# State-space scan: u written in the place of h, third banks of psX and psW, state sums for four units at a time

## The reference, cut to what matters

```
xz = x @ in_proj.T;  xc, z = split(xz)              # 512 inner channels
xs = silu(causal_conv4(xc) + conv_b)
dt_r, B, C = split(xs @ x_proj.T)                   # 16 + 16 + 16
dt = softplus(dt_r @ dt_proj.T + dt_b)
a = exp(dt[..., None] * A)                          # 16 states for a channel
u = dt[..., None] * B[:, :, None, :] * xs[..., None]
h[t] = a[t] * h[t-1] + u[t]                         # along the 2048 steps of a row
y = sum_s(h * C) + xs * D_skip;  y = y * silu(z)
out = y @ out_proj.T
```

## Time and profile before

| | |
|---|---|
| median of 3 runs | 3406.47 us (3404.86 to 3411.97) |
| the profiled execution | 3401.26 us, span 3399.5 us |
| busy over the span | PE 94%, DVE 82%, ACT 68%, POOL 47% |
| state-space loop, 2296 to 3382 us | PE 1034.9, DVE 980.6, ACT 782.2, POOL 888.5 us busy of 1086.0 |
| mean granted clock of TensorE | 0.977 of full speed |

### The profile page before, as it was taken

One profiled execution on the slowest core, in us unless ns is written; L12 is line 12 of the kernel. 1 busy time (PEld: TensorE's weight loads), 2 busy tenths in 40 slices (PEclk: granted clock), 3 DMA queues, 4 the chain that ended last, 5 costly groups with the idle time before them and its releaser, 6 DMA issues. The chain is left out here.

```text
span 3399.5 us, 61118 instructions
## 1 busy us (share of the span) xinstructions
PE 3188.7 (94%) x19814; PEld 1279.1 (38%) x19815; DVE 2788.6 (82%) x4945; ACT 2316.7 (68%) x3660; POOL 1601.0 (47%) x2080
## 2 busy tenths in 40 slices
PE   7997999989999999999999999769999999999987
PEld 4654666632222222222222222343334334333333
DVE  6766334689999999999999999258899989898997
ACT  4444333358887887888788788657877767777763
POOL 2113300024444434444333444207888888888885
PEclk9999999989999999999999999889999999999998
DMA  5442211111111110111111010141222222222221
GB/s 169 131 151 91 78 56 53 48 42 29 53 45 40 39 34 27 31 36 36 36 33 34 25 34 27 46 136 59 69 75 81 71 73 69 73 87 66 76 78 50
DMA packets 160889, 211.63 MB, mean 62 GB/s; under 512 B 32324, under 2 KB 108364, under 8 KB 160604
## 3 DMA queue, kind: packets, MB, share of 16 engines
q1 hardware_dynamic: 141340, 172.51, 16.6%
q0 software_dynamic: 8512, 18.76, 1.8%
q10 hardware_dynamic: 10752, 16.78, 1.5%
HBM read 154.48 MB, written 52.69 MB: 61 GB/s over the span
## 5 line engine op out<-in xcount | busy, mean ns | idle before, releaser
L1439 ACT ACTIVATE prob<-psS 128x1024 f32<-128x1024 f32 (+3 forms) x1280 | 1104.0, 906 | 280.2 <-PE psS L1623 270.8
L1489 DVE TENSOR_REDUCE pmax<-psR 128x1 f32<-128x512 f32 x1674 | 1057.2, 684 | 79.9 <-PE psR L1565 47.6
L2265 POOL TENSOR_TENSOR hc<-h_d,crep 128x512 f32<-128x512 f32 x512 | 647.7, 1273 | 186.8 <-DVE h_d L2494 136.5
L1565 PE MATMUL psR<-kslab,qslab 48*128 48x512 bf16 (+3 forms) x2480 | 653.0, 352 | 22.2 <-DVE pmax L1489 14.0
L1638 PE MATMUL psVo<-prob,vaug 128*32 128x512 f32 (+3 forms) x5120 | 630.8, 546 | 1.5 <-ACT ov L1443 0.8
L1623 PE MATMUL psS<-qslab,kslab 51*128 51x512 bf16 (+3 forms) x2560 | 533.4, 353 | 39.8 <-ACT prob L1439 22.6
L2494 DVE TENSOR_TENSOR_SCAN h_d<-a,state,psU 128x512 f32<-128x512 f32 x384 | 489.4, 1275 | 0.0
L1354 POOL TENSOR_SCALAR_AFFINE_SELECT prob<-prob 128x256 f32<-128x256 f32 (+1 forms) x512 | 214.0, 421 | 533.1 <-ACT prob L1439 533.1
L2484 DVE TENSOR_TENSOR psU<-dtx,psX 128x512 f32<-128x512 f32 x512 | 356.0, 695 | 89.6 <-PE psX L2644 38.8
L1565 PEld LDWEIGHTS psR<-kslab,qslab 48*128 48x128 bf16 x2480 | 187.3, 94 | 628.9 <-DVE pmax L1489 473.6
L2397 ACT ACTIVATE a<-dt,a_neg 128x512 f32<-128x512 f32 x512 | 366.7, 723 | 54.5 <-DVE h_d L2494 53.6
(11 more groups left out here) (351 smaller groups left out, 5045.5 us busy)
## 6 DMA issues: line engine op xcount, KB each, us to landing
crep<-c_rows_d SPq DMA_DIRECT2D x256, 256.0 KB, 3.1
x_e<-rows_d SPq DMA_DIRECT2D x72, 128.0 KB, 2.0
y_d<-y SPq DMA_DIRECT2D x72, 128.0 KB, 1.7
q_d<-parts SPq DMA_DIRECT2D x48, 128.0 KB, 2.4
k_d<-parts SPq DMA_DIRECT2D x48, 128.0 KB, 2.3
qslab<-q_d SPq DMA_DIRECT2D x60, 96.0 KB
kslab<-k_d SPq DMA_DIRECT2D x60, 96.0 KB
wg<-n_L_ffn_gate_proj_w_dram ACTq DMA_DIRECT2D x8, 512.0 KB, 4.1
```

The lines of the kernel that those rows point to most:

```text
L1439: act.activation(prob[g % BUFS][:, :, off:BLK], psS[g % 2][:, :, off:BLK], ACT.Exp).then_inc(prob_ready, 1)
L1489: dve.tensor_reduce(into[:, lo:lo + (count - 1) * NEXT + 1:NEXT], psR[at % BANKS][:, 0:count * w].rearrange("p (n w) -> p n w", w=w), AX.X ...
L1565: ins = pe.matmul(dst[:, m * w:(m + 1) * w], qslab[u][rows, i * P:(i + 1) * P], kslab[u][rows, ch * BLK:ch * BLK + w], start=(m == 0), sto ...
L2265: pool.tensor_tensor(hc[:, g % CR], h[:, g % HR], crep[:, g // PAIR % SPR], ALU.mult).then_inc(hc_ready, 1)
```

## The change

- u is written into the ring place of h (SBUF) in place of psU (PSUM), and the scan reads and writes that place. The waits for POOL's hc and for the kept state go from `scan(g)` to `input_term(g)`; the wait of u for the scan two before falls away. psU is gone.
- `HR` is 6 in place of 5 and `SPR` 3 in place of 4.
- psX and psW have three banks each in place of two (`XR`, `WR`); `places()` hands out three.
- `add_states` is called for two pairs at once, at each fourth unit, behind one wait for the fourth hc.
- One semaphore `log_chain` in place of ab_ready, ex_ready and ln_ready, with the counts worked out (`LOGS` = 4 steps for two tiles).

```
-        AR, HR, CR, LAG, SPR = 5, 5, 6, 3, 4
+        AR, HR, CR, LAG, SPR = 5, 6, 6, 3, 3
+        XR, WR = 3, 3
+        LOGS = PAIR + 2
...
-        psU = [ps(f"psU{i}", [P, BLK]) for i in range(2)]
-        psX = [ps(f"psX{i}", [P, BLK]) for i in range(2)]
-        psW = [ps(f"psW{s}", [P, BLK]) for s in range(2)]
+        psX = [ps(f"psX{i}", [P, BLK]) for i in range(XR)]
+        psW = [ps(f"psW{s}", [P, BLK]) for s in range(WR)]
...
-                s = 0 if until[0] <= until[1] else 1
+                s = until.index(min(until))
...
             def input_term(g):
...
-                if g >= 2:
-                    dve.wait_ge(h_ready, g - 1 + CREDIT)
-                dve.tensor_tensor(psU[g % 2][:], dtx[:, c], psX[g // PAIR % 2][:], ALU.mult).then_inc(u_ready, 1)
-
-            def scan(g):
-                blk, t, c, s = unit(g)
-                dve.wait_ge(a_ready, g + 1 + CREDIT)
                 if g >= HR:
                     dve.wait_ge(hc_ready, g - HR + 1 + CREDIT)
                     if unit(g - HR)[0] % BPB < BPB - 1:
                         dve.wait_ge(state_ready, kept(g - HR) + CREDIT)
+                dve.tensor_tensor(h[:, g % HR], dtx[:, c], psX[g // PAIR % XR][:], ALU.mult).then_inc(u_ready, 1)
+
+            def scan(g):
+                blk, t, c, s = unit(g)
+                dve.wait_ge(a_ready, g + 1 + CREDIT)
                 dve.wait_ge(u_ready, g + 1 + CREDIT)
-                dve.tensor_tensor_scan(h[:, g % HR], a[:, g % AR], psU[g % 2][:],
+                dve.tensor_tensor_scan(h[:, g % HR], a[:, g % AR], h[:, g % HR],
                                        0.0 if blk % BPB == 0 else state[:, c, s:s + 1],
                                        ALU.mult, ALU.add).then_inc(h_ready, 1)
...
-                if k >= 2:
-                    pe.wait_ge(u_ready, PAIR * (k - 1) + CREDIT)
-                pe.matmul(psX[k % 2][:], pick[:, k % NS:k % NS + 1].to_broadcast([3 * 2 * NS, P]),
+                if k >= XR:
+                    pe.wait_ge(u_ready, PAIR * (k - XR + 1) + CREDIT)
+                pe.matmul(psX[k % XR][:], pick[:, k % NS:k % NS + 1].to_broadcast([3 * 2 * NS, P]),
...
-                if g % PAIR == 0 and g > LAG:
-                    add_states((g - LAG) // PAIR)
+                if g % (2 * PAIR) == 2 and g > LAG + PAIR:
+                    pe.wait_ge(hc_ready, g - PAIR + CREDIT)
+                    for k in range(g // PAIR - 3, g // PAIR - 1):
+                        add_states(k)
```

More of the change, by code:

```diff
@@ L2032, in phase_state_space @@
         xl_ready = sem("d_xl_ready")
-        full = [sem(f"d_full{s}") for s in range(2)]
-        free = [sem(f"d_free{s}") for s in range(2)]
+        full = [sem(f"d_full{s}") for s in range(WR)]
+        free = [sem(f"d_free{s}") for s in range(WR)]
         state_ready = sem("d_state_ready")
@@ L2042, in phase_state_space @@
         xs_ready = sem("d_xs_ready")
-        ab_ready = sem("d_ab_ready")
-        ex_ready = sem("d_ex_ready")
-        ln_ready = sem("d_ln_ready")
+        log_chain = sem("d_log_chain")
         dt_ready = sem("d_dt_ready")
@@ L2112, in places @@
         def places():
-            got, count, until = {}, [0, 0], [0, 0]
+            got, count, until = {}, [0] * WR, [0] * WR
             def take(item, at, end):
-                s = 0 if until[0] <= until[1] else 1
+                s = until.index(min(until))
                 count[s] += 1
@@ L2226, in step_size @@
             def step_size(nb, c):
-                pool.wait_ge(ln_ready, 2 * nb + c // PAIR + 1 + CREDIT)
+                pool.wait_ge(log_chain, LOGS * (2 * nb + c // PAIR + 1) + CREDIT)
                 pool.tensor_tensor(dt_[:, c], dt_[:, c], cv[:, c % PAIR], ALU.add).then_inc(dt_ready, 1)
@@ L2361, in split_step @@
                     act.wait_ge(dtx_ready, CT * (nb - 1) + c + 1 + CREDIT)
-                act.activation(cv[:, c % PAIR], psW[s][:], ACT.Abs, bias=vec[:, 1, c:c + 1]).then_inc(ab_ready, 1)
+                act.activation(cv[:, c % PAIR], psW[s][:], ACT.Abs, bias=vec[:, 1, c:c + 1]).then_inc(log_chain, 1)
                 act.activation(dt_[:, c], psW[s][:], ACT.Relu, bias=vec[:, 1, c:c + 1]).then_inc(free[s], 1)
             def log_exp(nb, pair):
-                act.wait_ge(ab_ready, CT * nb + PAIR * (pair + 1) + CREDIT)
-                act.activation(cv[:], cv[:], ACT.Exp, scale=-1.0).then_inc(ex_ready, 1)
+                act.wait_ge(log_chain, LOGS * (2 * nb + pair) + PAIR + CREDIT)
+                act.activation(cv[:], cv[:], ACT.Exp, scale=-1.0).then_inc(log_chain, 1)
             def log_term(nb, pair):
-                act.wait_ge(ex_ready, 2 * nb + pair + 1 + CREDIT)
+                act.wait_ge(log_chain, LOGS * (2 * nb + pair) + PAIR + 1 + CREDIT)
                 for c in range(PAIR * pair, PAIR * pair + PAIR):
@@ L2373, in log_term @@
                     act.wait_ge(free[s], n + CREDIT)
-                act.activation(cv[:], cv[:], ACT.Ln, bias=1.0).then_inc(ln_ready, 1)
+                act.activation(cv[:], cv[:], ACT.Ln, bias=1.0).then_inc(log_chain, 1)
             def high_part(nb, kind, f):
@@ L2528, in _ @@
             for c in range(PAIR):
-                dve.wait_ge(ln_ready, 1 + CREDIT)
+                dve.wait_ge(log_chain, LOGS + CREDIT)
                 dve.tensor_tensor(dt_[:, c], dt_[:, c], cv[:, c], ALU.add).then_inc(dt_ready, 1)
```

## The result

The changed kernel takes 3669.67 us (median of 4 runs, 3665.90 to 3670.15) against 3405.66 us for the kernel before (median of 4, 3397.06 to 3411.97): 1.078 times as long, 95% interval 1.076 to 1.080. That is 264 us more. The forecast was 3768 us, 362 us more than before, in a range of 3440 to 3940.

The account below looks back on a forecast made before the run. The loop was taken as a near tie of DVE, pacing most stretches at 2.00 us a unit, and PE. Only the hold counted, +362 us, the other parts nothing: 3768 us from the median 3406.47, range 3440 to 3940.

Parts of the forecast that it names:

- The hold (part 1): State-space loop: a scan with both inputs in SBUF and POOL's SBUF-reading instructions exclude each other; +362 us, chance 0.72.
- I take the middle of 232 and 493: Size of the loop's hold: the middle of the two bounds, 362 us more, taken as the forecast.
- The lower end: Only the element-streaming parts of scans and POOL instructions exclude each other: loop of 1318 us, 232 us more.
- The upper end: Whole spans of scans and POOL instructions exclude each other, plus 0.09 us per unit: 1579 us, 493 us more.
- the row of the held tensor_scalar: Start of the experts' stage: a DVE tensor_scalar took 1.60 us, otherwise 0.58, ending where a POOL memset ended.
- What would show it: Loop signs: scan or hc 1.9 to 2.4 us, spans not overlapping, PE share 0.7, scan to scan 2.6 to 3.1 us.
- part 2: Loop waits for hc and kept state move from scan to u, 0.6 us earlier; priced at nothing.
- part 4: Loop sums of states for four units: 128 groups in place of 256, 33 us less of PE; nothing under the hold.
- rival C: No hold, but POOL's hc waits for late sums at each fourth unit: 3406 us, no change; 0.04 with the rest.
- part 5: Third psX and psW banks take PE's 14.3 + 9.1 us of buffer waits; worth nothing under the hold.
- Parts 3 and 6: SPR 4 to 3 leaves a crep row 5 us over; three log semaphores made one keep the waits; both zero.
- Rival A: The loop's scan isn't held, so PE's 33 us saving decides: 3373 us, chance 0.17.

Follow-up runs that it names:

- experiment 1: The kernel before with u alone written into h's place in SBUF and scanned there, rings, banks and sums as before: 3666.73 us, ratio 1.077.
- 3: The changed kernel with POOL's product hc replaced by a memset of the same place, so hc is written and h not read: 3389.22 us, ratio 0.996.
- 4: The changed kernel with a in two PSUM banks in place of SBUF, psX and psW back at two banks each: 3494.53 us, ratio 1.026.
- 8: The kernel of experiment 1 with a in two PSUM banks, sums for two units as before: 3443.41 us, ratio 1.013.
- 10: The kernel of experiment 1 with hc over 256 of 512 columns, half of the product with C left out: 3473.63 us in one run.
- experiment 2: The kernel before with the sums of states for four units at a time and nothing else: 3445.99 us, ratio 1.012.
- experiment 11: The kernel of experiment 7 with each u waiting again for the scan two before it: 3404.87 us, ratio 1.0003.
- 12: The kernel of experiment 7 unchanged, run again beside experiment 11 on one chip: 3389.77 us, ratio 0.996.
- experiment 7: The kernel before with a third bank of psX, u still in PSUM, odd u in psX itself without a wait for a scan: 3393.81 us, ratio 0.997.
- 9: The kernel before with sums for four units, seven places of hc, and the third psX bank of experiment 7: 3392.67 us, ratio 0.997.

## Why the prediction was right, and where it wasn't

**The hold (part 1): right, shown.** u alone in h's place costs 263 us (experiment 1); take the reading from POOL (3) or one of the scan's two tensors from SBUF (4, 8) and the scan is at 1277 ns again. The rule cited from the Trainium skill ("SBUF — State Buffer", section "Who interferes with whom"), that a DVE instruction with two SBUF inputs contends with a GpSimd instruction that reads SBUF and not with one that only writes it, is borne out by 1644 against 1278 ns. Its second half, that the loser blocks fully, agrees for the scan of 5.21 us behind three hc. In the steady stretch a scan and an hc together take 2.15 us, less than the 2.55 us of their two unstretched spans, so there the measurement speaks against a block of whole instructions.

**The size of the hold: 362 us forecast, 264 measured.** The step is the term "I take the middle of 232 and 493". The lower end, the streaming parts alone, gives a loop of 1318 us; the loop took 1353, of which POOL was idle for 24. In the steady stretch scan and hc take 2.15 us together; the step's parts, 1.26 - 0.15 and 1.27 - 0.19, make 2.19. The upper end had the whole spans and 0.09 us between each scan and its hc. The runs show neither: the 2.15 us leave room for the streaming parts alone, so the fixed part of the one must run beside the other's streaming, and POOL, always behind, waits for scans 9.9 us in the whole loop, not 46. The half-width hc (10) points the same way, in one run and 6 us outside its range. The scan's fixed part, 0.15 us, is borrowed from the product and was not measured. A held stretch should have been priced by its streaming part; the row of the held tensor_scalar only seemed to leave that open.

**What would show it:** the scan at 1.65 us and 1.71 in the mean, a little under the 1.9 to 2.4 given; both sides stretched, where the text let one be; 2.15 us from scan to scan in the steady stretch and 2.64 over the loop, the low end of the 2.6 to 3.1 given. Three signs came out otherwise: the recorded spans of scan and hc still overlap (1.65 and 2.18 us within 2.15), PE's busy share is 0.81 and not 0.7, and u is at 656 ns in the median, not 690. PE's clock did fall, from 0.98 to 0.89 of full speed over the loop, and with it PE's busy time rose from 1035 to 1101 us for the same matmuls. One group, after PE had stood for 5.10 us, ran at a granted clock of 0.50, the lower level of 1.2 GHz:

```profile
2626.25 3.69 PE L2658 MATMUL psYd<-hc,ident 64*64 64x512 f32 x16 [5.10 <-POOL hc L2264]
```

A like group at full clock takes 1.95 us (experiment 2, 2618.12). I read the fall of the clock as a consequence, not a cause. No run tries it, but POOL stands idle for only 24 us of the loop in all, so a slower PE can't have cost more than about that.

**The waits that move (part 2): wrong, and hidden.** Part 2 priced them at nothing and passed over the one that falls away. It stood between a scan and the u right behind it and cost 0.2 us a unit; removed from half of the units it gave 15 us (11 against 12) where 256 x 0.2 us would be 51; DVE then waits longer for PE (74.0 us for psX against 41.1). In the changed kernel the gain is lost in the hold.

**Sums for four (part 4): wrong in sign.** The sixteen take 1.9 us from the first to what follows, as forecast, but PE's busy time fell by 19 us with seven places (the sums' own by 25), where 33 were forecast. What failed is the other side: "POOL has two or three instructions to do meanwhile, 2.5 us or more" took PE to be at its place in time. In experiment 2 PE's matmuls wait for hc for 9.8 us only, and its weight loads for 39.9 us (63.8 before), while POOL waits 160.8 us for their sums: it is PE that comes late, itself busy for 92% of the loop, and the kernel loses 43 us. This is rival C, which had been given no more than the loss of A's gain. In the changed kernel POOL is slower than PE and its wait for psYd is 4.8 us, so this is hidden too.

**Third banks (part 5):** no gain from the third bank of psX that experiment 11 could test, which is released later than the change's. The change's own third banks, of psX and of psW, were not tried by themselves.

**Parts 3 and 6** at nothing: consistent with experiment 1, which has neither and takes the same time within 3 us; what they would be worth without the hold was not tried.

**Rival A** was right about one thing. Without the hold there was a gain to be had, though of 8 to 14 us and not 33 (experiments 7, 9 and 12), and it came from a wait that the rival doesn't name.

## What to carry to other kernels

Before a tensor moves from PSUM to SBUF, or the other way, write down for each instruction on VectorE how many of its inputs will lie in SBUF and whether GpSimd reads SBUF meanwhile. If two and yes, add the streaming parts of both engines and compare the sum with the span of the stage: here it is 1318 against 1086 us, and 1353 was measured. If two engines of a stage are both near the bound, expect a saving on one of them to be worth little more than the distance to the other. Sums made in larger groups need a longer ring of what they add: here one more place took back 43 us.

## What the runs showed of the hardware that wasn't expected

- A DVE instruction that waits by semaphore for the one right ahead of it starts 1.38 to 1.40 us after a scan's start, without the wait 1.19 us: 0.2 us for a wait on an engine that runs in order anyway (experiments 7 and 11). The wait also shows in the instruction's own duration: the odd u, with the same banks as source and target, takes 695 ns in the mean where it waits (experiment 11) and 676 ns where it doesn't (experiment 7); into SBUF, without the wait, 656 ns in the median (the changed kernel).
- The hold takes from both sides: in the steady stretch every scan is at 1.65 us in place of 1.27 and hc at 2.18 in the median in place of 1.27. But where POOL has several instructions ready, it may run three of them in a row at 1.24 us each while a scan waits. What decides between the two patterns stays open.
